# A graph network's preparation stage: edge loads on two queues, the row terms as a 126th column, digits stored in two halves, and vector work placed between gathers

## What is computed

```python
edge_index = jnp.stack([src, dst])
h = jnp.maximum(_layernorm(x, axis=-1), 0.0)
x = x + _L0_gnn_ref(h, src, dst, L0_gnn_W, L0_gnn_a)          # attention over the edges
h = jnp.maximum(_layernorm(x, axis=-1), 0.0)
x = x + _L1_gnn_ref(h, edge_index, L1_gnn_W, L1_gnn_b)        # three convolutions
h = jnp.maximum(_layernorm(x, axis=-1), 0.0)
x = x + _L2_gnn_ref(h, edge_index, ...)                       # five recurrent steps, then a small MLP
h = jnp.maximum(_layernorm(x, axis=-1), 0.0)
x = x + _L3_gnn_ref(h, edge_index, edge_weight, ...)          # weighted sum over neighbours
```

## Time and profile before

| | us |
|---|---|
| median of three executions | 2424.9 |
| the profiled execution | 2423.62 |
| its span in the profile | 2421.8 |
| `prepare`: start of the span to the first transfer of `counts` | 117.94 |
| DMA WT<-lists in the chain that ended last | 47% of the span |

### The profile page before, as it was taken

The page is one execution under the profiler, slowest core; times in us unless marked ns, Lnnn a source line. Parts: engine busy times, 40 slices in busy tenths (PEclk is TensorE's granted clock), DMA queues, the critical chain, the costliest instruction groups (busy, mean ns, idle before and its releaser), DMA issues.

```text
span 2421.8 us, 27777 instructions
## 1 busy us (share of the span) xinstructions
PE 2189.1 (90%) x10036; PEld 1209.9 (50%) x10037; DVE 1039.5 (43%) x2911; ACT 772.9 (32%) x1403; POOL 626.8 (26%) x432
## 2 busy tenths in 40 slices
PE   4599968988859997798999999999999999998998
PEld 3344458555525554344445554555445544464444
DVE  5499979999944456232112212122121211112202
ACT  2377767878833324121111101111111111112200
POOL 2000000000014433233444344443444344441000
PEclk9799965999989998899999999999999999999999
DMA  5200064434421112333222222223122322136582
GB/s 160 103 9 11 10 186 124 132 130 161 161 64 1 1 31 41 89 56 77 45 35 41 63 48 30 46 42 85 22 34 43 75 32 30 22 61 177 209 302 99
DMA packets 178644, 186.94 MB, mean 77 GB/s; under 512 B 101996, under 2 KB 165646, under 8 KB 174443
## 3 DMA queue, kind: packets, MB, share of 16 engines
q1 hardware_dynamic: 108474, 134.46, 17.6%
q0 software_dynamic: 56784, 1.28, 7.1%
q10 hardware_dynamic: 13260, 49.53, 5.7%
HBM read 100.83 MB, written 84.40 MB: 76 GB/s over the span
## 4 chain that ended last, share of the span: by engine, by line
DMA 48%; PE 7%; issue 4%; DVE 0%; ACT 0%; ACTq 0%; DVEq 0%; POOLq 0%
DMA WT<-lists 47%; PE banks L1798 6%; PE banks L1754 1%; DMA out_dram<-big 0%; PE banks L1763 0%; DMA lists<-scatD 0%; PE banks L1816 0%; PE banks L1779 0%; DVE big L2013 0%; ACT big L1890 0%; PE banks L1813 0%; ACT big L1927 0%; PE banks L1771 0%; DVE big L2015 0%; ACT big L1904 0%
## 5 line engine op out<-in xcount | busy, mean ns | idle before, releaser
L867 POOL DMA_INDIRECT WT<-lists x391 | 607.2, 1553 | 874.9 <-DMA WT<-lists 860.7
L1676 PE MATMUL banks<-big,feat 125*128 125x500 f16 (+1 forms) x3150 | 606.1, 353 | 19.4 <-DMA feat<-hnD 15.0
L1676 PEld LDWEIGHTS banks<-big,feat 125*128 125x128 f16 x3150 | 306.3, 97 | 309.3 <-DMA feat<-hnD 15.8
L1701 PE MATMUL banks<-H,U 128*128 128x500 f32 (+1 forms) x756 | 302.6, 541 | 10.0 <-issue 10.0
L1701 PE MATMUL banks<-aT,V 128*128 128x500 f32 (+1 forms) x756 | 296.4, 538 | 3.1 <-DVE HN L1969 3.1
L1701 PEld LDWEIGHTS banks<-aT,V 128*128 128x128 f32 x756 | 143.1, 190 | 145.0 <-issue 97.2
L1701 PEld LDWEIGHTS banks<-H,U 128*128 128x128 f32 x756 | 142.5, 191 | 139.8 <-issue 101.6
L1957 DVE SCALAR_TENSOR_TENSOR HN<-banks,bh,HN 128x500 f32<-128x500 f32 (+1 forms) x70 | 47.8, 682 | 377.4 <-ACT HN L1859 354.1
L1859 ACT ACTIVATE HN<-banks,bs 128x500 f32<-128x500 f32 (+1 forms) x70 | 44.4, 635 | 381.4 <-PE banks L1701 381.4
L1319 PE MATMUL banks<-big,G 125*128 125x500 f16 (+1 forms) x700 | 143.7, 364 | 23.0 <-DVE G L1409 23.0
L1082 PE MATMUL banks<-work 125*128 125x500 f32 (+1 forms) x350 | 157.5, 564 | 7.5 <-DMA work<-xhD 5.9
(11 more groups left out here) (301 smaller groups left out, 2288.8 us busy)
## 6 DMA issues: line engine op xcount, KB each, us to landing
big<-WT ACTq DMA_DIRECT2D x25, 1562.5 KB, 7.8
WT<-zero SPq DMA_DIRECT2D x39, 980.0 KB, 9.5
hTD<-HN SPq DMA_DIRECT2D x40, 250.0 KB
hnD<-stg SPq DMA_DIRECT2D x32, 250.0 KB
feat<-hnD SPq DMA_DIRECT2D x4, 2000.0 KB
H<-hTD SPq DMA_DIRECT2D x16, 500.0 KB
work<-xhD SPq DMA_DIRECT2D x28, 250.0 KB
WT<-lists POOLq DMA_INDIRECT x391, 3.0
```

Source lines behind the costliest of these rows:

```text
L867: nc.gpsimd.indirect_dma_start(out=WT, out_offset=bass.IndirectOffsetOnAxis(ap=lists[:, 0, t - first:t - first + 1], axis=0), in_=lists[:, ...
L1676: last = nc.tensor.matmul(SUMS[s % 2][half][:, 0:wid(ch)], rows_, A[:, j, cols(ch)], start=(j == 0 and part == 0), stop=(j == T - 1 and pa ...
L1701: last = nc.tensor.matmul(PS[bank][:, 0:w], wt_[:, kt, g:g + 128], v[:, kt, 0:w], start=(n == 0), stop=(n == len(terms) - 1))
```

## The change

It does seven things.

1. SP loads dst, then `ew`, then `wihN`; ACT loads src, W and x. VectorE waits for dst and src alone; TensorE waits for `ew` by a counter of its own. The other weights (`gWN`, `whhN`, `l0N`, `l1N`, `w12N`) move from ACT's queue to SP's, behind the store of `nearD`.
2. `ub` has 126 columns: the 125 equal ones and a 126th that gives `s_src`. `feature_row` writes 126 partitions, `trow` keeps 126, and the 25 one-column products (L430) and the copy of `scol` go. In `counts` SP stores row 126 of `trow` in DRAM (`sD`, 12.5 KB), waits for that, and loads it as `scol`, 125 partitions by 25 elements of 4 bytes.
3. The digits are stored in two halves: digits 4 to 7 as soon as they are there (`UPPER`), ahead of `xhD`, and digits 0 to 3 behind it (`DIGITS`).
4. On VectorE the 20 remaining statistics and the split of the edge weights come ahead of the wait for `found`; the scale and shift come ahead of the wait for `gathered`.
5. The two blocks of ones are filled by GpSimd, after its gathers are issued.
6. The copies of `trow` stand between the digits' instructions.
7. TensorE and ScalarE do `folded` up to 13 (before: 9) ahead of the gathers; ScalarE does `affine(0)` ahead of the copies of `wcol`.

```diff
+        def loads(eng, arr, to, arrived):
...
             def _(sp):
...
+                loads(sp, dst, ei[:, 1], eloaded)
+                loads(sp, ew, we, ew_in)
+                sp.dma_start(wihN[:], wih.rearrange("(a p) m -> p a m", p=128)).then_inc(w_in, 16)
                 sp.wait_ge(dve_did, EDGES)
                 sp.dma_start(nearD.rearrange("(g t e) o -> t g (e o)", g=EG, t=LANE), near1[:]).then_inc(cs_out, 16)
+                sp.dma_start(gWN[:], gW.rearrange("l (a p) m -> p (l a) m", p=128)).then_inc(g_in, 16)
+                sp.dma_start(whhN[:], whh.rearrange("(a p) m -> p a m", p=128)).then_inc(rest_in, 16)
...
+                sp.wait_ge(dve_did, UPPER)
+                sp.dma_start(digits[:, :, 4:8], made_digits[:, :, 4:8]).then_inc(outs, 16)
                 sp.wait_ge(h_r, SC)
                 sp.dma_start(xhD, h[:]).then_inc(outs, 16)
                 sp.wait_ge(dve_did, DIGITS)
-                sp.dma_start(digD.rearrange("(g t) k s e -> t g (k s e)", g=EG), dig[:].rearrange("t g k s e -> t g (k s e)")).then_inc(outs, 16)
-                sp.wait_ge(outs, 16 * 6)
+                sp.dma_start(digits[:, :, 0:4], made_digits[:, :, 0:4]).then_inc(outs, 16)
+                sp.wait_ge(outs, 16 * 7)
...
-                    nc.tensor.matmul(PS[(0, 5)[ch % 2]][0:P, 0:w], ub[:, 1, :], hT[:, ch * CH:ch * CH + w], start=True, stop=True).then_inc(tr_t, 1)
+                    nc.tensor.matmul(PS[(0, 5)[ch % 2]][0:P + 1, 0:w], ub[:], hT[:, ch * CH:ch * CH + w], start=True, stop=True).then_inc(tr_t, 1)
...
-                for j in range(T):
-                    last = nc.tensor.matmul(PS[7][0:P, j:j + 1], hT[:, j * P:(j + 1) * P], ub[:, 0, 0:1], start=True, stop=True)
-                last.then_inc(tr_t, 1)
...
             def _(act):
+                loads(act, src, ei[:, 0], eloaded)
                 act.dma_start(aWN[:, 0, :], aW).then_inc(loaded, 16)
                 act.dma_start(xn[:], x.rearrange("(k p) d -> p k d", p=P)).then_inc(x_in, 16)
-                act.dma_start(wihN[:], wih.rearrange("(a p) m -> p a m", p=128)).then_inc(w_in, 16)
...
+                act.wait_ge(dve_did, SCALED)
+                affine(0)
                 for b in range(SPAN):
                     act.wait_ge(gath_t, b + 1)
...
             def _(sp):
-                for b in range(NBATCH):
-                    if b >= RD:
-                        sp.wait_ge(gap_r, b - RD + 1)
+                sp.dma_start(sD, trow[P:P + 1, :]).then_inc(outs, 16)
+                for b in range(RD):
+                    sp.dma_start(dig[:, b].rearrange("k t s e -> k t (s e)"), digD[b * BATCH:(b + 1) * BATCH].rearrange("t k s e -> k t (s e)")).then_inc(d_in[b], 16)
+                sp.wait_ge(outs, 16)
+                sp.dma_start(scol, sD.rearrange("o (j p) -> p (o j)", p=P), allow_slow_non_contiguous=True).then_inc(outs, 16)
+                for b in range(RD, NBATCH):
+                    sp.wait_ge(gap_r, b - RD + 1)
                     sp.dma_start(dig[:, b % RD].rearrange("k t s e -> k t (s e)"), digD[b * BATCH:(b + 1) * BATCH].rearrange("t k s e -> k t (s e)")).then_inc(d_in[b % RD], 16)
```

More of the change, by code:

```diff
@@ L124, in gnn_kernel @@
                         digD, nearD, VD, whhD, l0D, l1D, w12D, xhD)
-                counts(nc, sem, PS, banks, A, edges, digD, scatD, WT)
-            attention(nc, sem, PS, x, aW, xhD, x1D, xh1D, A, trow, ident, identh, col, scat_sems, scatD, WT)
+                counts(nc, sem, PS, banks, A, edges, sD, digD, scatD, WT)
+            attention(nc, sem, PS, x, aW, xhD, x1D, xh1D, A, trow[0:P], ident, identh, col, scat_sems, scatD, WT)
         with ExitStack() as c1:
@@ L242, in prepare @@
         dve_did = sem("dve_did")
-        EDGES, CS, ABC, CAND, TILES_, ROWS, REP, LESS, SCALED, DIGITS = range(1, 11)
+        EDGES, CS, ABC, CAND, TILES_, ROWS, REP, SCALED, LESS, UPPER, DIGITS = range(1, 12)
         MADE, ALL = 7, 17
@@ L394, in _ @@
                 pe.wait_ge(w_c, len(jobs))
-                for i in range(EARLY, 10):
+                for i in range(EARLY, LATE):
                     folded(i)
@@ L413, in _ @@
                     last.then_inc(gath_t, 1)
-                for i in range(10, LATE):
-                    folded(i)
                 pe.wait_ge(gath_c, SPAN)
@@ L490, in _ @@
                                    PS[6 + b % 2][:].rearrange("p (a r) -> p a r", a=2)).then_inc(gath_c, 1)
-                for i in range(10, LATE):
-                    folded(i)
-                act.wait_ge(dve_did, SCALED)
-                affine(0)
                 for ch in range(SC):
@@ L567, in _ @@
                 done(V_.tensor_scalar(tl[:], tl[:], float(LANE), None, ALU.mult))
-                spread(5, 15)
+                spread(5, T - 1)
+                done(V_.bn_stats(stats[:, T - 1, :], xn[:, T - 1, :]))
+                dve.wait_ge(edge_c, EG)
+                w = ecol[:, 3]
+                V_.tensor_copy(wp[:, :, 3], rank[:].bitcast(f32).to_broadcast([128, EG * LANE]))
+                left = [a[:].rearrange("p g e -> p (g e)") for a in (near, part)]
+                done(V_.tensor_copy(wp[:, :, 0], w))
+                for q in range(2):
+                    done(V_.tensor_tensor(left[q], w, wp[:, :, q], ALU.subtract))
+                    w = left[q]
+                    done(V_.tensor_copy(wp[:, :, q + 1], w))
                 dve.wait_ge(made, ALL)
@@ L593, in _ @@
                 V_.tensor_copy(rep[:], cover[:, :, :, None].to_broadcast([128, 3, WH, LANE])).then_inc(dve_did, 1)
-                spread(15, T - 1)
-                done(V_.bn_stats(stats[:, T - 1, :], xn[:, T - 1, :]))
+                for j in range(T):
+                    last = V_.bn_aggr(mv[:, j, :], stats[:, j, :])
+                done(last)
+                done(V_.tensor_scalar(st[:, 0, :], mv[:, :, 1], EPS, None, ALU.add))
+                root(V_, done, st[:, 2, :], st[:, 0, :], st[:, 1, :])
+                V_.scalar_tensor_tensor(st[:, 3, :], mv[:, :, 0], -1.0, st[:, 2, :], ALU.mult, ALU.mult).then_inc(dve_did, 1)
                 dve.wait_ge(gathered, 16 * SB)
@@ L605, in _ @@
                 V_.tensor_copy(gk, gtmp[:]).then_inc(dve_did, 1)
-                for j in range(T):
-                    last = V_.bn_aggr(mv[:, j, :], stats[:, j, :])
-                done(last)
-                done(V_.tensor_scalar(st[:, 0, :], mv[:, :, 1], EPS, None, ALU.add))
-                root(V_, done, st[:, 2, :], st[:, 0, :], st[:, 1, :])
-                V_.scalar_tensor_tensor(st[:, 3, :], mv[:, :, 0], -1.0, st[:, 2, :], ALU.mult, ALU.mult).then_inc(dve_did, 1)
                 dve.wait_ge(row_t, 1)
@@ L665, in _, with counts @@
                 done(V_.tensor_scalar(tmp[:], tmp[:], -ROUND, 64.0, ALU.add, ALU.mult))
+                rows_of(4, 5)
                 V_.tensor_copy(digit(0, 0), tmp[:])
                 V_.tensor_copy(digit(1, 2), tmp[:])
+                rows_of(5, 6)
                 V_.tensor_tensor(digit(0, 1), sq[:, :, 0], tmp[:], ALU.subtract)
                 V_.tensor_tensor(digit(1, 3), sq[:, :, 0], tmp[:], ALU.subtract).then_inc(dve_did, 1)
-                for ch in range(SC):
-                    dve.wait_ge(tr_t, ch + 1)
-                    V_.tensor_copy(trow[:, ch * CH:ch * CH + wid(ch)], PS[(0, 5)[ch % 2]][0:P, 0:wid(ch)]).then_inc(tr_c, 1)
-                dve.wait_ge(tr_t, SC + 1)
-                V_.tensor_copy(scol, PS[7][0:P, 0:T])
-def counts(nc, sem, PS, banks, A, edges, digD, scatD, WT):
+                rows_of(6, SC)
+def counts(nc, sem, PS, banks, A, edges, sD, digD, scatD, WT):
     with ExitStack() as c:
@@ L684, in sb @@
             return c.enter_context(nc.sbuf_tensor(name, shape, dt))
[L686 to L687 removed]
+        scol, trow, comb, sib, keyc, wc, wp, rank, wcol, visits, pairs, nodes, first, place, past, dump = (edges[n] for n in (
+            "scol", "trow", "comb", "sib", "keyc", "wc", "wp", "rank", "wcol", "visits", "pairs", "nodes", "first", "place", "past", "dump"))
         ohp = sb("ohp", [128, 2, SPAN, WC], f16)
```

102 lines of the change are left out of this document (52 added, 50 removed).

## The result

The changed kernel takes 2410.81 us (median of 6 runs, 2409.5 to 2413.62), the kernel before 2427.75 in the same comparison: a ratio of 0.9933, 95% interval 0.9918 to 0.9949. The forecast was 2413. The profiled execution has a span of 2411.2 us, 10.6 less than before.

The account below looks back on a forecast made before the run. The path was taken to be edges, x, two rounds of gathers, seven chunks, then `xhD`'s transfer and what queues behind it. Eight terms summed to -11.6 us, from 2424.9 to 2413 us, range 2405 to 2420.

Parts of the forecast that it names:

- Front, +7.5: Start of `prepare`: statistics of x begin at 34.3 us instead of 26.82, since the weights' loads slow x; +7.5 us.
- Rival A: Load of x: hardly slowed by the weights, lands at 24.1 us; -21.8 us, 2403 us in all; chance 0.18.
- `TILES_`, `ROWS`, `gathered`, `LESS`: Successive VectorE stretches from the statistics of x to `LESS`: -0.5, +1.2, 0 and 0 us.
- Step 3: `TILES_` to `ROWS`: VectorE's 8.8 us of moved work outlasts the gathers' 7.6 us landing; +1.2 us.
- Step 4: `ROWS` to `gathered`: 4.3 us of small VectorE work fits in the wait for the second gathers; 0 us.
- To `xhD`, -17.8: `LESS` to the issue of `xhD`: chunks run without the `trow` wait, 16.9 us instead of 34.7; -17.8 us.
- rival C: Chunks: do not run free (4 us each), or the tail does not shrink and x is late; 2422 us; chance 0.15.
- Tail, -3.0: Issue of `xhD` to start of `counts`: half the digits stored earlier, 1.05 MB less behind `xhD`; -3.0 us.
- `counts`, +1.0: Start of `counts`: storing `scol`'s row and loading its 3125 small elements ahead of the digit loads; +1 us.
- Rival B: Start of `counts`: `scol`'s elements, 92 ns each, block the fourth digit load; +33 us, 2458 us; chance 0.12.
- D: Front: src and dst on two queues land no sooner; changes nothing, since x is later; no chance given.

Follow-up runs that it names:

- weights_behind_x: Changed kernel with the weights' loads moved back to ACT's queue behind x; 2405.78 us in one execution.
- x_spread: Changed kernel with x loaded in two pieces, 120 and 5 partitions; 2400.42 us, 0.989 of the kernel before.
- vector_order_before: Changed kernel with the moved VectorE work (ten statistics, scale and shift, weight split, ones) and ScalarE's first normalization put back; 2417.34 us, 0.9965 of the kernel before.
- edges_one_queue: Changed kernel with src loaded on SP's queue again, behind dst; 2410.74 us in one execution.
- late_spread_two: late_spread with xhD's first 16 of 25 tiles stored as soon as they are made; 2390.92 us, 0.9856 of the kernel before.
- late_spread: Changed kernel with all statistics of x behind `rep`, and x's load and xhD's store each split into 120 and 5 partitions; 2394.13 us, 0.987 of before.
- rows_after_digits: Changed kernel with all copies of `trow` behind the digits again; 2419.04 us, 0.9959 of the kernel before.
- digits_whole: Changed kernel with the digits stored in one piece behind xhD; 2410.07 us in one execution.

## Why the prediction was right

The time and the sign came out, and so did seven of the eight terms, within 1.5 us; the tail did not. The errors partly cancel: the front and the chunks were 2.8 us too good in the sum, the tail and `counts` 3.3 us too bad.

1. *Front, +7.5: was +8.9.* The mechanism was right: VectorE's early start is lost in the wait for x, x takes turns with the weights on a few engines, and `weights_behind_x` and `x_spread` each give some 11 us of its landing back. The size rested on the weights running at full rate on x's engines; x landed 1.5 us later than that, well inside the bounds of 24.1 and 39.4. Rival A is dead: with 74 packets a us beside the weights, x was slowed to less than half of its 185.
2. *`TILES_`, `ROWS`, `gathered`, `LESS`: within 0.1 us of forecast each.* Step 3 said that VectorE's 8.8 us of work would be late and not the gather, at 7.6. It was a draw: in this profile the gather landed 8.8 us after `TILES_`, 0.19 after VectorE was free, in `vector_order_before` after 7.8, in `edges_one_queue` after 9.9. So the number rests in part on luck. Step 4 said that its cover has some 3 us to spare: the wait left is 3.33.
3. *To `xhD`, -17.8: was -16.4.* TensorE has no wait for `trow` but 0.69 us at the end: rival C is dead. What the sum overlooked is TensorE's clock: it took every time from rows at the full clock, and the change itself makes TensorE idle for 9.03 us ahead of the chunks. The gathers and their copies take 3.5 us, not 2.6, and the five intervals, five times 2.45 in the sum, are 4.2, 2.9, 2.4, 2.4 and 0.8. The last is short because its chunk has one tile, so the 1.4 us missed are the slow start less this. `late_spread_two` beside `late_spread` puts the slow start at some 2.4 us. `rows_after_digits` and `vector_order_before` show that the term is not one edit's: taken back alone, they cost 5.0 and 4.4 us at T, under the 9 to 10 and 6 that I had put on them.
4. *Tail, -3.0: was -5.3.* This is the step that was mis-sized. The half of the digits ahead is worth 2.7 (`digits_whole`), about the 3.0 given to it, but the picture behind the 3.0 was wrong, and that the two numbers meet is luck: the step took the half as bytes at the full rate of all engines, and the rows show a queue on `xhD`'s five, which first pass the features (0.24 MB in 2 us) and then their share of the digits. An estimate from that: five sixteenths of 1.05 MB at 0.12 MB a us are 2.7 us. The remaining 2.6 us are in no term, and their cause is not shown. Two things differ in the rows. The last digits go out 5.9 us behind `xhD` and not at once; in `rows_after_digits`, where they go out at once, the tail is 1.1 us longer. And the last store of `VD` goes out 1.6 us behind `xhD` (at 86.95) where it was 6.8 before (98.93); no run tried that alone.
5. *`counts`, +1.0: was 0.* 850 elements a us, where the bound of 92 ns each would have meant 54. Rival B's price rested on a row whose time belonged to other loads, as the prediction argued against it. The trace of before could have said so: in 986:990, where that load ran, its queue's 633 packets took 8.5% of 16 engines, 8.6 ns each, while the other queue held 60.1%.
6. *D holds*: `edges_one_queue` costs 0.3 us at T, too little to tell from nothing.
7. *Not foreseen*: 1.5 us given back in later blocks. The sum of the terms was -11.6, at T it was -12.1, in the span -10.6, in the comparison of medians -16.9 (0.67%, interval 0.51% to 0.82%, that is 12 to 20 us). The 6.3 us between the last two are the choice of executions: the profiled one of before lies 4.1 us under its median of 2427.75, the profiled one after 2.2 above its own.

What the change itself leaves is the largest finding: the statistics of x stand ahead of the gathers' tiles though nothing there needs them, and x uses a third of the engines. The edits to that, with the spread and early stores, are worth about as much again as the whole change. The next one would be to keep TensorE from idling ahead of the chunks; no run tried it.

## What to carry over

Before a load is put beside another, look at how many engines it runs on: a share of 16 engines near a third, with nothing else on its way, may say that the number of partitions divides badly, and a split into a well-divisible piece and a rest may be worth more than any order of queues. Put work that waits for a late load behind the issue of the next long transfer, not ahead of it. When a wait is taken off one engine, do the sum per engine again: two edits that fill the same wait are not worth the sum of the two. And when work is moved ahead on TensorE, ask whether it idles afterwards, and at which clock the rows were taken from which the next stretch is summed.

## What the runs showed of the hardware

- A transfer of 4-byte elements is cheaper than I had bounded it: 1700 of them in 2 us (in 109:111), the packets' times adding up to 47.8% of 16 engines, 9.0 ns each. The Trainium skill, "DMA: Bandwidth & Descriptors", Measured, gives a floor of about 10.5 ns a packet, for loads that GpSimd issues; the trace is under it. All 3125 elements pass in some 3.7 us, where the prediction's estimate by that floor was 6.6.
- Two queues on the same engines take turns badly for the one with small packets: x fell from 185 to 61 packets a us (122 in 2 us, 16:18) while the other queue kept 96.6% of the engines' time.
- Stores of 12.8 KB rows spread over 15 engines reach 200 to 250 KB a us, 1.7 to 2.1 times what they reach on 5; a packet takes 0.95 to 0.78 us instead of 0.51.
- TensorE's granted clock was 0.50 for 7 us after an idle time of 9.03 us, and the same four products took 2.77 us instead of 1.46. After 2.71 us (`rows_after_digits`) it was 0.50 too; after 2.39 (`late_spread`) 0.54, and after 2.22 (`late_spread_two`) 1.00.
- An engine that issues a transfer can be held in it: SP's L335 took 6.88 us to issue beside full queues, where such an issue takes 0.3 to 0.7 us. I see no cost of it here: the engines' waits on the path do not name the loads behind it.

```profile
7.02 6.88 SPq L335 DMA_DIRECT2D big<-in_L_gnn_w_hh_dram  x1
```
